# A feed-forward stage with quantized weights: dequantize before the matmul, or scale after it

## The chip, the cores and the metric

The kernel runs on one core of one Trainium2 chip. A core has five engines with queues of their own: TensorE (PE, matmuls into PSUM), VectorE (DVE), ScalarE (ACT), GpSimd (POOL, no PSUM here) and SyncE (SP, which issues the loads). The metric is the device time of the whole program in microseconds (us), lower is better. Before the change it is 1844.55 us, the median of three runs (1840.67 to 1845.38).

## What is computed

Two decoder layers on x of 8 batches x 128 tokens x 512 features: six sub-layers, each followed by a residual and a layer norm. The change is in the third, a feed-forward with weights kept as integers 0 to 15 and a zero and a scale for each group of 128 input features and each output column:

```
def dequantize(imatrix, scales, zeros, group_size, out_dtype):
    rs = jnp.repeat(scales, group_size, axis=0)
    rz = jnp.repeat(zeros, group_size, axis=0)
    return ((imatrix.astype(rs.dtype) - rz.astype(rs.dtype)) * rs).astype(out_dtype)
gate = jax.nn.silu(jnp.dot(x, gate_proj))      # 512 -> 1792
up = jnp.dot(x, up_proj)                        # 512 -> 1792
return jnp.dot(gate * up, down_proj)            # 1792 -> 512
x = _layernorm(x + _L0_ffn_ref(x, ...), axis=-1)
```

The group size 128 is also the depth of one matmul: 512 input features are four groups, c = 0 to 3.

## The kernel before

The program is six stages behind one another (hydra, cross0, ffn0, self, cross1, lora), with a barrier of all engines between them. The tokens stay in SBUF as m.xtok (tokens on partitions) and transposed as m.xT_hi and m.xT_lo, each number split into a high part of the matmul's reduced fp32 format and a low rest. `three` (L69 to 73) multiplies a high/low pair by a high/low pair with three matmuls and leaves out low times low.

The ffn0 stage (L1246, `ffn0_stage`) walks the 1792 inner features in 7 turns of 256. In a turn SP loads integers, zeros and scales of gate and up (six transfers of 512 KB, the zeros and scales copied to all partitions) and of down (three more). DVE subtracts the zeros (L1370, L1373), POOL multiplies by the scales (L1302, L1304), DVE makes the high part (L1378, L1383) and POOL the low part (L1308, L1310). A turn has four units: 128 inner features by 512 tokens each. In a unit PE runs the gate chain and the up chain, 4 groups x 3 matmuls each, into two pairs of banks; ACT takes silu of gate out of PSUM (L1352), DVE multiplies it by up (L1391, h), ACT copies the high part of h (L1358), DVE subtracts for the low part (L1396). After the four units PE multiplies h by the down weights, 8 batches x 2 halves of the turn x 3 matmuls of 512 columns, and DVE adds each batch's rows to m.xtok (L1405).

All turns after the first are a hardware loop on each engine. DVE's order in a turn sets when the weights of the next turn are made: behind the second unit. Semaphores name who waits for whom; nothing is scheduled by a planner.

At the end `norm_vector`, `norm_gpsimd`, `norm_tensor` and `norm_scalar` (L84 to 124) normalize: all eight batches' statistics, then one reciprocal root for all on POOL, then batch by batch scaling (DVE), transposing (PE), high copy (ACT), low subtraction (DVE). The cross0 stage before uses another form, one batch at a time: `batch_stats`, `batch_rstd`, `batch_scale`, `batch_turn`, `batch_high`, `batch_low` (L1428 to 1464).

m.pre is a buffer of 16 KB a partition for early loads. It serves the first two stages (`PREFETCHED = 2`, L1929) and is then given back. In cross0 SP loads the output weights in four parts into it, and POOL's splits (`split_q`, `split_o`) free it; its last use ends near 477 us, and that stage near 571.

## Time and profile before

| what | us |
|---|---|
| median of three runs | 1844.55 |
| the profiled execution, whole | 1839.86 |
| its span | 1838.0 |
| PE busy in the span | 1597.0 (87%) |
| DVE, ACT, POOL busy | 903.7, 726.9, 681.5 |
| ffn0: first load issued | 571.55 |
| ffn0: first matmul, last output row added | 598.98, 842.13 |
| ffn0: last low half of the norm | 861.55 |

Times inside the program count from the span's start. A matmul's busy time overlaps with its neighbours', since they are pipelined; the distance between their starts is what each costs. An operation on ACT, DVE or POOL also overlaps the next one of its engine a little. A time with an arrow behind it says how long the engine was idle before, and who ended the wait.

### The profile page before, as it was taken

How to read it: one execution, taken by the hardware profiler on the slowest of the kernel's cores; microseconds unless marked ns; L12 is line 12 of the kernel's file. 1: busy time of each engine (PE TensorE's matmuls, PEld its weight loads, DVE VectorE, ACT ScalarE, POOL GpSimd, SP SyncE). 2: the span in 40 equal slices, each digit the busy share in tenths (PEclk: the TensorE clock that was granted, in tenths of full speed). 3: DMA queues.
4: the chain of work that ended last, by engine and by line, in shares of the span. 5: the costliest groups of instructions: out<-in, count | busy, mean ns of one | idle time of the engine just before them, and what ended most of it. 6: DMA issues, size and time to landing. Idle time of an engine off the chain costs nothing. (4 is left out here: it accounts for less than half of the span.)

```text
span 1838.0 us, 29158 instructions
## 1 busy us (share of the span) xinstructions
PE 1597.0 (87%) x10870; PEld 1323.4 (72%) x10870; DVE 903.7 (49%) x1547; ACT 726.9 (40%) x2318; POOL 681.5 (37%) x498
## 2 busy tenths in 40 slices
PE   5888899999992999995699855999999999999846
PEld 3757687888871777773677634888888888888734
DVE  0726512333374455445256762555555555555744
ACT  2131224444441111111499952454445554445400
...
GB/s 189 35 0 0 49 13 26 19 34 5 2 2 140 169 103 166 142 0 62 82 1 2 47 8 120 26 34 47 35 36 31 28 47 35 24 1 1 1 41 46
DMA packets 70718, 84.93 MB, mean 46 GB/s; under 512 B 14080, under 2 KB 50304, under 8 KB 70592
## 3 DMA queue, kind: packets, MB, share of 16 engines
...
## 5 line engine op out<-in xcount | busy, mean ns | idle before, releaser
L984 POOL TENSOR_TENSOR xa_rs<-xa_ms,minus_half 128x5 f32<-128x5 f32 x64 | 74.8, 1169 | 171.1 <-DVE xa_ms L1206 171.1
L967 POOL TENSOR_TENSOR xa_prob<-xa_prob,xa_inv 128x512 f32<-128x512 f32 x64 | 66.6, 1041 | 138.7 <-DVE xa_inv L1173 138.7
L1151 ACT ACTIVATE xa_prob<-xa_prob,xa_peak 128x128 f32<-128x128 f32 x256 | 100.3, 394 | 42.5 <-DVE xa_peak L1217 42.5
L600 POOL TENSOR_TENSOR xa_prob<-xa_prob,xa_inv 128x1024 f32<-128x1024 f32 x32 | 60.7, 1896 | 141.2 <-DVE xa_inv L854 141.2
L1201 DVE TENSOR_REDUCE xa_ssq<-xa_qn 128x4 f32<-128x512 f32 x64 | 43.9, 686 | 136.7 <-ACT xa_qn L1137 136.7
L71 PE MATMUL xa_qp<-xa_q_hi,xT_hi 128*128 128x512 f32 x256 | 108.4, 423 | 2.0 <-DVE xa_q_lo L1164 2.0
L1741 ACT ACTIVATE sa_work<-sa_work,sa_peak 128x128 f32<-128x128 f32 x256 | 99.8, 399 | 21.2 <-DVE sa_peak L1778 21.1
L71 PE MATMUL xa_rows<-xa_o_hi,xa_out_hi 128*128 128x512 f32 x256 | 101.6, 397 | 5.2 <-DVE xtok L1180 5.2
L72 PE MATMUL xa_qp<-xa_q_hi,xT_lo 128*128 128x512 f32 x256 | 102.4, 400 | 0.0
L73 PE MATMUL xa_rows<-xa_o_lo,xa_out_hi 128*128 128x512 f32 x256 | 102.0, 398 | 0.0
L73 PE MATMUL xa_qp<-xa_q_lo,xT_hi 128*128 128x512 f32 x256 | 101.8, 398 | 0.0
L72 PE MATMUL xa_rows<-xa_o_hi,xa_out_lo 128*128 128x512 f32 x256 | 101.6, 397 | 0.0
L1577 POOL TENSOR_TENSOR sa_work<-sa_work,sa_inv 128x1024 f32<-128x1024 f32 x32 | 60.7, 1898 | 106.0 <-DVE sa_inv L1782 105.9
L1352 ACT ACTIVATE ff_act_g<-ff_gate 128x512 f32<-128x512 f32 x28 | 16.8, 600 | 209.8 <-PE ff_gate L73 209.8
L836 DVE TENSOR_REDUCE xa_peak<-xa_score 128x4 f32<-128x1024 f32 x32 | 39.2, 1224 | 114.3 <-PE xa_score L678 114.3
L1137 ACT ACTIVATE xa_qn<-xa_qp 128x512 f32<-128x512 f32 x64 | 38.3, 598 | 143.0 <-PE xa_qp L73 143.0
L71 PE MATMUL xa_kvp<-xa_kv_hi,cT_hi 128*128 128x256 f32 x256 | 78.7, 308 | 8.6 <-DVE xa_kv_lo L1159 8.6
L73 PE MATMUL xa_kvp<-xa_kv_lo,cT_hi 128*128 128x256 f32 x256 | 73.3, 286 | 0.0
L72 PE MATMUL xa_kvp<-xa_kv_hi,cT_lo 128*128 128x256 f32 x256 | 73.1, 286 | 0.0
L1034 PEld LDWEIGHTS xa_score<-xa_kT,xa_qT 128*128 128x128 f32 x512 | 66.9, 191 | 6.6 <-ACT xa_qT L1117 1.2
L71 PE MATMUL ff_gate<-xT_hi,ff_gu_hi 128*128 128x512 f32 x112 | 45.2, 404 | 29.8 <-POOL ff_gu_lo L1308 29.8
L1302 POOL TENSOR_TENSOR ff_gu_w<-ff_gu_w,ff_gu_s 128x2048 f32<-128x2048 f32 x7 | 37.8, 5398 | 86.2 <-DVE ff_gu_w L1370 86.2
...
## 6 DMA issues: line engine op xcount, KB each, us to landing
...
```

What stands on the lines that cost most here:

```text
L71: pe.matmul(out, a_hi, b_hi, start=first, stop=False)
L72: pe.matmul(out, a_lo, b_hi, start=False, stop=False)
L73: return pe.matmul(out, a_hi, b_lo, start=False, stop=last)
L600: pool.tensor_tensor(prob[:, t % 3, :, :], prob[:, t % 3, :, :], bc(inv[:, t % 3, :], 2, [P, Q, KEYS]), ALU.mult).then_inc(s["norm"], 1)
L836: dve.tensor_reduce(peak[:, t % 3, :], score4[:, :, 0:KEYS], AX, ALU.max, negate=True).then_inc(s["peak"], 1)
L967: pool.tensor_tensor(prob[:, u % 2, :, :], prob[:, u % 2, :, :], bc(inv[:, u % 2, :], 2, [P, Q, S]), ALU.mult).then_inc(s["norm"], 1)
L984: pool.tensor_tensor(rs[:, :], ms[:, :], m.minus_half[:, 0:Q + 1], ALU.pow).then_inc(s["rs"], 1)
L1034: last = pe.matmul(score[:, h * P:(h + 1) * P], qT[:, h, :], kT[:, :], start=True, stop=True)
L1151: last = act.activation(prob[:, u % 2, h, :], prob[:, u % 2, h, :], ACT.Exp, bias=peak[:, u % 2, h:h + 1], accum_out=total[:, u % 2, h:h + 1])
L1201: dve.tensor_reduce(ssq[:, 0:Q], qn[:, :, :], AX, ALU.add).then_inc(s["ssq"], 1)
L1577: pool.tensor_tensor(prob[:, u % 3, :, :], prob[:, u % 3, :, :], bc(inv[:, u % 3, :], 2, [P, HC, S]), ALU.mult).then_inc(s["norm"], 1)
L1741: last = act.activation(prob[:, t % 3, h, :], prob[:, t % 3, h, :], ACT.Exp, bias=peak[:, t % 3, h:h + 1], accum_out=total[:, t % 3, h:h + 1])
```

## The change

The gate and up weights are no longer scaled before the matmul. DVE subtracts the zeros and writes the integers (-15 to 15) straight into the matmul's format, where they are exact, so they need no low part. PE multiplies a group's integers by the high and the low x: 2 matmuls into a bank of their own, and so 8 groups a unit (4 gate, 4 up) in a ring of 6 banks. The scale of a group and an inner feature is then a column, one number a partition: the scales are loaded small and transposed once by PE (`sT`). ACT takes the even groups out of PSUM with the scale (`part`), DVE the odd ones with the scale and adds them to ACT's (`part`), POOL adds the two sums of gate and the two of up (`total`), ACT takes silu, POOL multiplies (`product`), ACT copies the high part (`high`), POOL subtracts the low part (`low`). The output rows of a turn are multiplied during the next turn's units, one batch in the middle of a unit and one at its end (`mid`, `end`), with the rest in `drain`; h therefore has two places, for which the idle m.cT buffers serve. The down weights are dequantized as before, but in smaller pieces. The loads of turn 0 are issued by SP in the cross0 stage into m.pre, which is kept one stage longer. The norm is done batch by batch. All hardware loops are written out.

The lines removed are the body of `ffn0_stage` as printed above. The lines added, with inner parts moved left, and without plain allocations:

```diff
+    ffn_scales(sp, io, m.scales, s["ld_next"])
+    sp.wait_ge(s["split_q"], PIECES_Q * Q)
+    sp.wait_ge(s["split_o"], PIECES_O * Q)
+    ffn_stage_inputs(sp, io, *ffn_stage_buffer(m.pre), 0, s["ld_next"])
+    sp.wait_ge(s["ld_next"], 96)
...
+def ffn_stage_inputs(sp, io, dest_q, dest_z, g, done):
+    cols = slice(g * WIDE, (g + 1) * WIDE)
+    for n, w in enumerate(("gate", "up")):
+        sp.dma_start(dest_q[:, :, n, :], io[w + "_w"].rearrange("(c p) n -> p c n", p=P)[:, :, cols]).then_inc(done, 16)
+        sp.dma_start(dest_z[:, :, n, :], io[w + "_z"][:, cols].partition_broadcast(P)).then_inc(done, 16)
+def ffn_stage_buffer(flat):
+    return [flat[:, n * KC * 2 * WIDE:(n + 1) * KC * 2 * WIDE].bitcast(INT32).rearrange("p (c a n) -> p c a n", c=KC, a=2) for n in range(2)]
+def ffn_scales(sp, io, dest, done):
+    for n, w in enumerate(("gate", "up")):
+        sp.dma_start(dest[n * KC * TILES:(n + 1) * KC * TILES, :], io[w + "_s"].rearrange("g (t n) -> (g t) n", n=P)).then_inc(done, 16)
 def ffn0_stage(nc, m, io, sem):
+    UNITS = 4 * TURNS
+    RING = 6
+    LAST = TURNS - 1
...
+        other = sb("other", [P, 2 * KC * 2 * WIDE])
+        stage = [ffn_stage_buffer(m.pre), ffn_stage_buffer(other)]
+        w = sb("w", [P, 2, KC, 2, WIDE], F32R)
...
+        acc = sb("acc", [P, 2, 4, HALF])
...
+        dn_hi, dn_lo = (sb(n, [P, 2, MT, D], F32R) for n in ("dn_hi", "dn_lo"))
+        h_hi, h_lo = (x[:, :, :].rearrange("p (a k) n -> p a k n", a=2) for x in (m.cT_hi, m.cT_lo))
...
+        mid, end, drain = {}, {}, []
+        for n in range(4, 4 * LAST):
+            g, j = n // 4, n % 4
+            mid[n], end[n] = [(g - 1, 2 * j)], [(g - 1, 2 * j + 1)]
+        n = 4 * LAST
+        for j in range(2):
+            mid[n + j] = [(LAST - 1, 4 * j), (LAST - 1, 4 * j + 1)]
+            end[n + j] = [(LAST - 1, 4 * j + 2), (LAST - 1, 4 * j + 3)]
+        end[n + 2], mid[n + 3], end[n + 3] = [(LAST, 0)], [(LAST, 1)], [(LAST, 2)]
+        drain = [(LAST, b) for b in range(3, B)]
+        def column(n, i):
+            t = MT * (n // 4) + n % MT
+            return sT[:, i // 4, i % 4, t:t + 1]
...
 @block.sync
...
+    for g in range(TURNS):
+        if g:
+            if g >= 3:
+                sp.wait_ge(s["w"], KC * (g - 2))
+            elif g == 2:
+                sp.wait_ge(s["w_first"], KC)
+            ffn_stage_inputs(sp, io, *stage[g % 2], g, s["ld_odd" if g % 2 else "ld_even"])
+            sp.wait_ge(s["dn_sub"], g)
+            sp.wait_ge(s["dn_w"], MT * g)
...
+        sp.dma_start(dn_q[:, :, :], io["down_w"].rearrange("(m p) n -> p m n", p=P)[:, part, :]).then_inc(s["ld_dn"], 16)
...
 @block.gpsimd
...
+    def low(n):
+        g, half, k = n // 4, n % 4 // 2, n % MT
+        cols = slice(half * HALF, (half + 1) * HALF)
+        pool.wait_ge(s["h_hi"], n + 1)
+        pool.tensor_tensor(h_lo[:, g % 2, k, cols], acc[:, n % 2, 2, :], raw(h_hi[:, g % 2, k, cols]),
+                           ALU.subtract).then_inc(s["h_lo"], 1)
+    def total(n, a):
+        pool.wait_ge(s["cd"], 4 * n + 2 + 2 * a)
+        pool.tensor_tensor(acc[:, n % 2, 2 * a, :], acc[:, n % 2, 2 * a, :], acc[:, n % 2, 2 * a + 1, :], ALU.add).then_inc(s["sum"], 1)
+    def product(n):
+        pool.wait_ge(s["silu"], n + 1)
+        pool.wait_ge(s["sum"], 2 * n + 2)
+        pool.tensor_tensor(acc[:, n % 2, 2, :], acc[:, n % 2, 0, :], acc[:, n % 2, 2, :], ALU.mult).then_inc(s["h"], 1)
+    for n in range(UNITS):
+        g, j = n // 4, n % 4
+        if n:
+            low(n - 1)
+        total(n, 0)
+        if j == 0:
+            pool.wait_ge(s["dn_sub"], g + 1)
+            for k in range(MT):
+                pool.tensor_tensor(dn_w[:, k, :], dn_w[:, k, :], dn_s[:, k, :], ALU.mult).then_inc(s["dn_w"], 1)
+        total(n, 1)
+        product(n)
+    low(UNITS - 1)
+    for b in range(B):
+        batch_rstd(pool, m, n2, b)
 @block.tensor
...
+    def group(n, i):
+        q = 8 * n + i
+        g, half, k, c, a = n // 4, n % 4 // 2, n % MT, i % 4, i // 4
+        cols = slice(half * HALF, (half + 1) * HALF)
+        if q >= RING:
+            pe.wait_ge(s["cd"] if i % 2 else s["ca"], (q - RING) // 2 + 1)
+        elif q == RING - 1:
+            pe.wait_ge(s["sT"], 1)
+        f = slice(k * P, (k + 1) * P)
+        bank = ring[q % RING]
+        pe.matmul(bank[:, :], w[:, g % 2, c, a, f], m.xT_hi[:, c, cols], start=True, stop=False)
+        pe.matmul(bank[:, :], w[:, g % 2, c, a, f], m.xT_lo[:, c, cols], start=False, stop=True).then_inc(s["grp"], 1)
+    def out_rows(g, b):
+        r = B * g + b
+        half = b // 4
+        pe.wait_ge(s["dn_lo"], MT * (g + 1))
+        pe.wait_ge(s["h_lo"], 4 * g + 2 * (half + 1))
+        if r >= 2:
+            pe.wait_ge(s["add"], r - 1)
+        for k in range(MT):
+            last = three(pe, rows[r % 2][:, :], h_hi[:, g % 2, k, b * P:(b + 1) * P], h_lo[:, g % 2, k, b * P:(b + 1) * P],
+                         dn_hi[:, g % 2, k, :], dn_lo[:, g % 2, k, :], k == 0, k == MT - 1)
+        last.then_inc(s["rows"], 1)
+    def turn(b):
+        if b == 0:
+            pe.wait_ge(s["cd"], 4 * UNITS)
+            pe.wait_ge(s["ca"], 4 * UNITS)
+        if b >= 2:
+            pe.wait_ge(n2["lo"], b - 1)
+        batch_turn(pe, m, n2, b, ring[b % 2][:, :])
+    pe.transpose(ring[RING - 1][:, 0:2 * KC * TILES], m.scales[0:2 * KC * TILES, :],
+                 m.ident[0:2 * KC * TILES, 0:2 * KC * TILES]).then_inc(s["sT_mm"], 1)
+    for n in range(UNITS):
+        g, j = n // 4, n % 4
+        if n == 0:
+            pe.wait_ge(s["w_first"], KC)
+        elif j == 0:
+            pe.wait_ge(s["w"], KC * g)
+        for i in range(4):
+            group(n, i)
+        for r in mid.get(n, ()):
+            out_rows(*r)
+        for i in range(4, 8):
+            group(n, i)
+        for r in end.get(n, ()):
+            out_rows(*r)
+    for n, r in enumerate(drain):
+        out_rows(*r)
+        if n:
+            turn(n - 1)
+    for b in range(len(drain) - 1, B):
+        turn(b)
 @block.scalar
...
+    def part(n, i):
+        act.wait_ge(s["grp"], 8 * n + i + 1)
+        act.activation(acc[:, n % 2, i // 2, :], ring[(8 * n + i) % RING][:, :], ACT.Copy, scale=column(n, i)).then_inc(s["ca"], 1)
+    def high(n):
+        g, half, k = n // 4, n % 4 // 2, n % MT
+        act.wait_ge(s["h"], n + 1)
+        if g >= 2:
+            act.wait_ge(s["rows"], B * (g - 1))
+        act.activation(h_hi[:, g % 2, k, half * HALF:(half + 1) * HALF], acc[:, n % 2, 2, :], ACT.Copy).then_inc(s["h_hi"], 1)
+    act.wait_ge(s["sT_mm"], 1)
+    act.activation(sT[:, :, :, :].rearrange("p a c t -> p (a c t)"), ring[RING - 1][:, 0:2 * KC * TILES], ACT.Copy).then_inc(s["sT"], 1)
+    act.wait_ge(s["sT"], 1)
+    for n in range(UNITS):
+        g, j = n // 4, n % 4
+        if n >= 2:
+            act.wait_ge(s["h_lo"], n - 1)
+        part(n, 0)
+        part(n, 2)
+        if n:
+            high(n - 1)
+        if j == 1:
+            for k in range(MT):
+                act.wait_ge(s["dn_w"], MT * g + k + 1)
+                if g >= 2 and k == 0:
+                    act.wait_ge(s["rows"], B * (g - 1))
+                act.activation(dn_hi[:, g % 2, k, :], dn_w[:, k, :], ACT.Copy).then_inc(s["dn_hi"], 1)
+        act.wait_ge(s["sum"], 2 * n + 1)
+        act.activation(acc[:, n % 2, 0, :], acc[:, n % 2, 0, :], ACT.Silu).then_inc(s["silu"], 1)
+        part(n, 4)
+        part(n, 6)
+    high(UNITS - 1)
+    for b in range(B):
+        batch_high(act, m, n2, b, ring[b % 2][:, :])
 @block.vector
...
+    def part(n, i):
+        dve.wait_ge(s["grp"], 8 * n + i + 1)
+        dve.wait_ge(s["ca"], 4 * n + i // 2 + 1)
+        dve.scalar_tensor_tensor(acc[:, n % 2, i // 2, :], ring[(8 * n + i) % RING][:, :], column(n, i), acc[:, n % 2, i // 2, :],
+                                 ALU.mult, ALU.add).then_inc(s["cd"], 1)
+    def add_rows(g, b):
+        r = B * g + b
+        dve.wait_ge(s["rows"], r + 1)
+        if g:
+            dve.wait_ge(s["add"], r - B + 1)
+        dve.tensor_tensor(m.xtok[:, b, :], m.xtok[:, b, :], rows[r % 2][:, :], ALU.add).then_inc(s["add"], 1)
+    q, z = stage[0]
+    for c in range(KC):
+        dve.tensor_tensor(w[:, 0, c, :, :], q[:, c, :, :], z[:, c, :, :], ALU.subtract).then_inc(s["w_first"], 1)
+    dve.wait_ge(s["sT"], 1)
+    for n in range(UNITS):
+        g, j = n // 4, n % 4
+        for r in end.get(n - 1, ()):
+            add_rows(*r)
+        if j == 0:
+            dve.wait_ge(s["ld_dn"], 48 * (g + 1))
+            if g:
+                dve.wait_ge(s["dn_lo"], MT * g)
+            dve.tensor_tensor(dn_w[:, :, :], dn_q[:, :, :], dn_z[:, :, :], ALU.subtract).then_inc(s["dn_sub"], 1)
+        part(n, 1)
+        part(n, 3)
+        if g < LAST:
+            q, z = stage[(g + 1) % 2]
+            if j == 0:
+                dve.wait_ge(s["ld_even" if g % 2 else "ld_odd"], 64 * ((g + 1) // 2 if g % 2 else g // 2 + 1))
+                dve.wait_ge(s["grp"], 32 * g)
+            dve.tensor_tensor(w[:, (g + 1) % 2, j, :, :], q[:, j, :, :], z[:, j, :, :], ALU.subtract).then_inc(s["w"], 1)
+        for r in mid.get(n, ()):
+            add_rows(*r)
+        part(n, 5)
+        part(n, 7)
+        if j == 1:
+            for k in range(MT):
+                dve.wait_ge(s["dn_hi"], MT * g + k + 1)
+                dve.tensor_tensor(dn_lo[:, g % 2, k, :], dn_w[:, k, :], raw(dn_hi[:, g % 2, k, :]), ALU.subtract).then_inc(s["dn_lo"], 1)
+    for r in end[UNITS - 1]:
+        add_rows(*r)
+    for b in range(B):
+        if b >= 3:
+            add_rows(LAST, b)
+        if b >= 5:
+            batch_low(dve, m, n2, b - 5, ring[(b - 5) % 2][:, :])
+        dve.wait_ge(s["add"], B * LAST + b + 1)
+        batch_stats(dve, m, n2, b)
+        if b:
+            batch_scale(dve, m, n2, b - 1)
+    batch_scale(dve, m, n2, B - 1)
+    for b in range(3, B):
+        batch_low(dve, m, n2, b, ring[b % 2][:, :])
...
-PREFETCHED = 2
+PREFETCHED = 3
```

## Rows read from the trace of the kernel before

**Rows 1.** table by stretches: length, busy (count) by engine, PE clock, DMA share, GB/s

```profile
540.00:566.00 26.00, 19.72 (x244) 15.29 (x244) 17.41 (x30) 9.23 (x19) 5.92 (x6) 1.00 0.01 2
...
566.00:599.00 33.00, 0.64 (x5) 0.44 (x5) 14.36 (x10) 1.88 (x2) 12.75 (x4) 0.56 0.65 211
...
735.00:770.00 35.00, 33.78 (x148) 27.43 (x147) 19.10 (x21) 4.60 (x8) 15.38 (x4) 1.00 0.42 140
...
842.00:862.00 20.00, 8.39 (x32) 5.86 (x32) 14.78 (x34) 4.79 (x8) 1.65 (x1) 0.60 0.00 0
```

**Rows 2.** groups by line, 530 to 920 us: busy, mean ns, idle before

```profile
L71 PE MATMUL ff_gate<-xT_hi,ff_gu_hi 128*128 128x512 f32 x112 | 45.2, 404 | 29.8 <-POOL ff_gu_lo L1308 29.8
...
L1358 ACT ACTIVATE ff_h_hi<-ff_h 128x512 fp32r<-128x512 f32 x28 | 17.6, 628 | 16.8 <-DVE ff_h L1391 16.8
...
L1569 POOL TENSOR_TENSOR xtok<-xtok,sa_bias_o 128x512 f32<-128x512 f32 x8 | 9.8, 1267 | 0.0
```

**Rows 3.** timeline, the stage's start: start, us, engine, line

```profile
571.55 0.39 SPq L1283 DMA_DIRECT2D ff_gu_q<-in_gate_w  x1
...
583.20 2.29 DVE L1370 TENSOR_TENSOR ff_gu_w<-ff_gu_q,ff_gu_z 128x2048 f32<-128x2048 int32 x1 [12.66 <-DMA ff_gu_s<-in_up_s]
...
587.03 4.11 DVE L1373 TENSOR_TENSOR ff_dn_w<-ff_dn_q,ff_dn_z 128x1024 f32<-128x1024 int32 x1 [1.54 <-DMA ff_dn_s<-in_down_s]
...
600.00 0.63 PE L73 MATMUL ff_gate<-xT_lo,ff_gu_hi 128*128 128x512 f32 x1
...
600.43 0.63 PE L71 MATMUL ff_gate<-xT_hi,ff_gu_hi 128*128 128x512 f32 x1
```

**Rows 4.** the product h of the feed-forward (ff_h): ns min/median/max, first and last start

```profile
L1391 DVE TENSOR_TENSOR ff_h<-ff_act_g,ff_up x28: 686/687/689, 607.1 to 830.2; 128x512 f32<-128x512 f32 x28
```

**Rows 5.** timeline, ACT in a turn, last high half, last low half

```profile
747.56 0.60 ACT L1352 ACTIVATE ff_act_g<-ff_gate 128x512 f32<-128x512 f32 x1 [4.89 <-PE ff_gate L73]
...
748.05 0.63 ACT L1358 ACTIVATE ff_h_hi<-ff_h 128x512 fp32r<-128x512 f32 x1
...
830.94 0.64 ACT L1358 ACTIVATE ff_h_hi<-ff_h 128x512 fp32r<-128x512 f32 x1 [2.40 <-DVE ff_h L1391]
...
860.86 0.69 DVE L100 TENSOR_TENSOR xT_lo<-ff_gate,xT_hi 128x512 fp32r<-128x512 f32 x1 [0.36 <-ACT xT_hi L122]
```

**Rows 6.** timeline, POOL with 128x512 operations

```profile
265.49 1.04 POOL L564 TENSOR_TENSOR xa_wide_hi<-pre,ones 128x512 fp32r<-128x512 f32 x1 [39.55 <-PE xa_score L73]
...
266.61 1.30 POOL L566 TENSOR_TENSOR xa_wide_lo<-pre,xa_wide_hi 128x512 fp32r<-128x512 f32 x1
...
893.29 9.84 POOL L1569 TENSOR_TENSOR xtok<-xtok,sa_bias_o 128x512 f32<-128x512 f32 x8
```

**Rows 7.** timeline, the norm of one batch

```profile
566.09 0.69 DVE L1430 BATCH_NORM_STATS2 stats<-xtok 128x6 f32<-128x512 f32 x1
...
567.04 0.15 DVE L1434 TENSOR_SCALAR var<-meanvar 128x1 f32<-128x1 f32 x1
...
567.27 0.55 POOL L1439 TENSOR_TENSOR rstd<-var,minus_half 128x1 f32<-128x1 f32 x1 [5.39 <-DVE var L1434]
...
567.86 0.55 DVE L1444 TENSOR_SCALAR xtok<-xtok,meanvar,rstd 128x512 f32<-128x512 f32 x1 [0.66 <-POOL rstd L1439]
```

**Rows 8.** groups by line, ACT: a copy without and with a column of scales

```profile
L1126 ACT ACTIVATE xa_v_hi<-xa_kvp 128x128 fp32r<-128x128 f32 x64 | 17.3, 270 | 0.0
...
L356 ACT ACTIVATE hy_yT<-hy_bank,hy_norm_w 128x128 f32<-128x128 f32 x32 | 9.5, 366 | 7.2 <-PE hy_bank L306 6.8
```

**Rows 9.** timeline, DVE and POOL in one turn

```profile
753.77 1.22 DVE L1373 TENSOR_TENSOR ff_dn_w<-ff_dn_q,ff_dn_z 128x1024 f32<-128x1024 int32 x1
...
753.93 5.55 POOL L1302 TENSOR_TENSOR ff_gu_w<-ff_gu_w,ff_gu_s 128x2048 f32<-128x2048 f32 x1 [10.85 <-DVE ff_gu_w L1370]
...
756.46 3.57 DVE L1396 TENSOR_TENSOR ff_h_lo<-ff_h,ff_h_hi 128x512 fp32r<-128x512 f32 x1
...
759.45 2.86 POOL L1304 TENSOR_TENSOR ff_dn_w<-ff_dn_w,ff_dn_s 128x1024 f32<-128x1024 f32 x1
```

More of the change, by code:

```diff
@@ L1258, in ffn0_stage @@
+        acc = sb("acc", [P, 2, 4, HALF])
         dn_q, dn_z = (sb(n, [P, MT, D], INT32) for n in ("dn_q", "dn_z"))
         dn_s, dn_w = (sb(n, [P, MT, D]) for n in ("dn_s", "dn_w"))
-        dn_hi, dn_lo = (sb(n, [P, MT, D], F32R) for n in ("dn_hi", "dn_lo"))
-        act_g = sb("act_g", [P, 2, HALF])
-        h = sb("h", [P, 2, HALF])
-        h_hi, h_lo = (sb(n, [P, MT, TOK], F32R) for n in ("h_hi", "h_lo"))
-        gate = [pb(f"gate{i}") for i in range(2)]
-        up = [pb(f"up{i}") for i in range(2)]
+        dn_hi, dn_lo = (sb(n, [P, 2, MT, D], F32R) for n in ("dn_hi", "dn_lo"))
@@ L1266, in ffn0_stage @@
+        h_hi, h_lo = (x[:, :, :].rearrange("p (a k) n -> p a k n", a=2) for x in (m.cT_hi, m.cT_lo))
+        ring = [pb(f"ring{i}") for i in range(RING)]
         rows = [pb(f"rows{i}") for i in range(2)]
-        m.norm_bank = gate
         s = {n: sem("ff_" + n) for n in (
-            "ld_gu", "ld_dn", "sub_gu", "sub_dn", "w_gu", "w_dn", "hi_gu", "hi_dn", "lo_gu", "lo_dn", "gate",
-            "up", "silu", "h", "h_hi", "h_lo", "rows", "add")}
+            "ld_even", "ld_odd", "ld_dn", "w_first", "w", "sT_mm", "sT", "grp", "ca", "cd", "sum", "silu", "h", "h_hi", "h_lo",
+            "dn_sub", "dn_w", "dn_hi", "dn_lo", "rows", "add")}
@@ L1297, in _ @@
             @block.gpsimd
             def _(pool):
-                def scale(g):
-                    pool.wait_ge(s["sub_gu"], g + 1)
-                    pool.tensor_tensor(gu_w[:, :, :, :], gu_w[:, :, :, :], gu_s[:, :, :, :], ALU.mult).then_inc(s["w_gu"], 1)
-                    pool.wait_ge(s["sub_dn"], g + 1)
-                    pool.tensor_tensor(dn_w[:, :, :], dn_w[:, :, :], dn_s[:, :, :], ALU.mult).then_inc(s["w_dn"], 1)
-                def low(g):
-                    pool.wait_ge(s["hi_gu"], g + 1)
-                    pool.tensor_tensor(gu_lo[:, :, :, :], gu_w[:, :, :, :], raw(gu_hi[:, :, :, :]), ALU.subtract).then_inc(s["lo_gu"], 1)
-                    pool.wait_ge(s["hi_dn"], g + 1)
-                    pool.tensor_tensor(dn_lo[:, :, :], dn_w[:, :, :], raw(dn_hi[:, :, :]), ALU.subtract).then_inc(s["lo_dn"], 1)
@@ L1312, in _ @@
-                scale(0)
-                low(0)
-                with pool.Fori(1, TURNS) as g:
-                    scale(g)
-                    low(g)
-                norm_gpsimd(pool, m, n2)
+                def low(n):
[4 more added lines that the diff above has]
+                                       ALU.subtract).then_inc(s["h_lo"], 1)
@@ L1319, in _ @@
+                low(UNITS - 1)
+                for b in range(B):
+                    batch_rstd(pool, m, n2, b)
             @block.tensor
             def _(pe):
-                def group(g):
-                    pe.wait_ge(s["lo_gu"], g + 1)
-                    for j in range(CHAINS):
-                        half, k = j // MT, j % MT
-                        cols = slice(half * HALF, (half + 1) * HALF)
-                        pe.wait_ge(s["h"], CHAINS * g + max(j - 1, 0))
-                        for n, (bank, done) in enumerate(((gate[j % 2], s["gate"]), (up[j % 2], s["up"]))):
-                            for c in range(KC):
-                                last = three(pe, bank[:, :], gu_hi[:, c, n, k * P:(k + 1) * P], gu_lo[:, c, n, k * P:(k + 1) * P],
-                                             m.xT_hi[:, c, cols], m.xT_lo[:, c, cols], c == 0, c == KC - 1)
-                            last.then_inc(done, 1)
-                    pe.wait_ge(s["lo_dn"], g + 1)
-                    for b in range(B):
-                        pe.wait_ge(s["h_lo"], CHAINS * g + MT * (b // 4 + 1))
-                        pe.wait_ge(s["add"], B * g + max(b - 1, 0))
-                        for k in range(MT):
-                            last = three(pe, rows[b % 2][:, :], h_hi[:, k, b * P:(b + 1) * P], h_lo[:, k, b * P:(b + 1) * P],
-                                         dn_hi[:, k, :], dn_lo[:, k, :], k == 0, k == MT - 1)
-                        last.then_inc(s["rows"], 1)
@@ L1346, in _ @@
+                for n, r in enumerate(drain):
[4 more added lines that the diff above has]
+                    turn(b)
             @block.scalar
             def _(act):
-                def group(g):
-                    for j in range(CHAINS + 1):
-                        if j < CHAINS:
-                            act.wait_ge(s["gate"], CHAINS * g + j + 1)
-                            act.activation(act_g[:, j % 2, :], gate[j % 2][:, :], ACT.Silu).then_inc(s["silu"], 1)
-                        if j:
-                            n = j - 1
-                            half, k = n // MT, n % MT
-                            act.wait_ge(s["h"], CHAINS * g + n + 1)
-                            act.wait_ge(s["rows"], B * g)
-                            act.activation(h_hi[:, k, half * HALF:(half + 1) * HALF], h[:, n % 2, :], ACT.Copy).then_inc(s["h_hi"], 1)
```

85 lines of the change are left out of this document (7 added, 78 removed).

## The prediction

> **What bounds the kernel now.** I read the table by stretches first, to see what the feed-forward stage is made of, then the groups by line, then the timelines of its start, one turn, and its end. The table [rows 1] shows four parts: 33 us in which PE works 0.64 us, a body in which PE is busy 33.78 of 35 us at the full clock, and 20 us at the end with PE busy 8.4. PE in the body is the bound: 148 matmuls in 33.78 us are 0.228 us each, and a turn of 144 makes 32.9 of its roughly 34.4. Every other engine there is at most 19 of 35 busy. The hole at the start ends with POOL: PE waited 29.8 us for ff_gu_lo [rows 2]. Its inside is the load, from 571.55 to 583.20, then subtract, scale, split and scale again in a row [rows 3]. The first product h begins at 607.1 and the last at 830.2, 27 units of (128 features x 512 tokens) later, 8.26 us each [rows 4]; the last low half of the norm ends at 861.55 [rows 5].
>
> **PE's share after the change.** A unit has 8 groups of 2 matmuls instead of 2 chains of 12, and still 12 for the output rows: 28 instead of 36. That is 28 x 0.228 = 6.4 us instead of 8.2, and over 28 units 51 us less. If PE stayed the bound, this would be the gain. I do not think it does, for the scales now cost ACT, DVE and POOL work on every group, and the order written for them closes a ring.
>
> **The ring.** Follow one unit from the end of product(n-1) on POOL. ACT does high(n-1); POOL may only then do low(n-1), and after it, in its order, total(n,0); ACT waits for that with silu(n) and only behind silu issues part(n,4) and part(n,6); DVE adds part(n,7); POOL does total(n,1) and product(n). Nothing in it can start a unit earlier, since each engine's order is fixed. The two parts 0 and 2 and DVE's 1 and 3 are done before and cost nothing. Prices:
> - high: 0.63 for SBUF to SBUF [rows 2], 0.04 from DVE's end (830.21 + 0.69) to ACT's start at 830.94 [rows 4, 5], taken for POOL to ACT as well: 0.67.
> - low and total(n,0): a 128x512 tensor operation of two SBUF operands on POOL is 1.26 [rows 2], and eight in a row took 9.84, so 1.225 from one start to the next. A POOL operation that waits for another engine starts 0.08 after that one's end (567.19 to 567.27) [rows 6, 7]. So 0.08 + 1.225 + 1.26 = 2.57.
> - silu, part 4, part 6: ACT's 128x512 takes 0.60 and the next starts 0.49 later [rows 5]. What a scale taken from a column adds is not shown at this size; at 128x128 it makes 366 ns of 270 [rows 8], so 0.10. Its cost lies between 0 and 0.2 a part; I take 0.10. So 0.04 + 0.53 + 0.60 + 0.70 = 1.87.
> - part 7 on DVE: 0.04 + 0.70, the 0.69 of a PSUM operation at this size [rows 4] and 0.01 for the column.
> - total(n,1): 0.08 + 1.26; product, which waits for POOL's own total: 1.12 from start to start where the operation took 1.04 [rows 6], so 0.08 + 1.25. Together 2.67.
> Sum: 0.67 + 2.57 + 1.87 + 0.74 + 2.67 = 8.5 us a unit. That is longer than PE's 6.4 and longer than the 8.26 of now. PE gets 2 us of idle per unit. With no column cost and every hand-over at its least it is 8.2, with 0.03 more at each of nine hand-overs 8.8.
>
> **What else is in a turn of four units.** POOL's two multiplications of dn_w (2 x 1.25) fall between total 0 and total 1, where POOL waits 2.7 us for ACT and DVE anyway: nothing. ACT's dn_hi falls in its wait for total 0: nothing. DVE's own sum is 4 parts, 2 additions of rows, 1 subtraction and a quarter of the dn work, some 5.4 of 8.5: not the bound. But DVE and POOL exclude one another when DVE has two SBUF operands: DVE's h_lo, 0.69 at other times, started at 756.46 and took 3.57, to 0.55 after POOL's 5.55 us operation ended at 759.48; and POOL's own next one, at 759.45, and that one before it, which met a DVE subtraction at 753.77, were each longer than their work [rows 9]. So DVE slips in between two POOL operations and pushes the later one. The new subtraction w (once a unit) is asked for 0.9 before product ends, waits, and runs in the 0.75 us while ACT does high: no cost. The dn subtraction (1.1 us, first unit of a turn) comes between total 1 and product: +1.05. The two dn_lo (second unit) come around total 1: +0.45 and +0.55, and the w after them meets low: +0.25. In 7 turns: 6 x 1.05 + 7 x 1.25 = 15. The bounds are 0, if every one falls into one of POOL's gaps, and 30, if all 24 w (0.6), 6 dn (1.1) and 14 dn_lo (0.6) displace POOL, less the first turn.
>
> **Start.** SP begins at 571.55 as now [rows 3], since the 2 MB of integers for turn 0 and the scales come in the stage before, behind the last weights, and land long before its end; PE there does not wait for them. DVE subtracts at once, PE can begin at 574. But DVE's order blocks it: before part 1 stands the dn load, three 512 KB transfers; they would be there at about 579.4, one step of three before the six and nine below. Then dn subtraction and parts 1 and 3, to 582. Then the w subtraction, which waits for turn 1's four transfers, the seventh in the queue; six were there at 583.20 and nine at 587.03, so 584.5 [rows 3]. Subtraction 0.6, parts 5 and 7 1.3, total and product 2.67: product(0) ends at 589.0. PE's cold start (0.43 us a matmul, 600.00 to 600.43) is hidden in that. Bounds 586 and 592.
>
> **End.** After product(27): high and low 2.1. Only then may POOL do rstd(0), for low stands ahead of it: 0.55 more. From there DVE is the chain. A batch costs it stats, aggregate and var 1.1, scale 0.55 [rows 7], row addition and low half 0.65 each: 2.95 in full. So 2.65 + 0.55 for scale 0, 1.6 for batch 1 and 2's rest, 2.25 twice, 2.95 three times, 1.2 for the last rstd and scale, 1.3 for two low halves that are ready, and 3.8 for the last three at the pace of transpose, copy and subtraction: 24.5. Now it is 30.7 from 830.9 to 861.55 [rows 4, 5]. Bounds 20 and 28.
>
> **Sum.** 589.0 + 27 x 8.52 (230) + 15 + 24.5 = 858.6 against 861.55: 3 us less. Loads in the stage before, longer straight code in place of loops, SP's longer list: nothing on the path, at most 2 us either way. The profiled execution has a span of 1838.0 and 1839.86 in all, 4.7 below the median 1844.55 of three; less 3 it is 1836.9, and on the median's scale 1841.6. I say 1841.
>
> **Rivals.**
> A. DVE never hurts POOL and the hand-overs are at their least: 27 x 8.2 = 221 instead of 245, and some 1 to 3 us off start and end: 22 to 28 us faster than my sum, 1815. For it: the w subtraction has 0.15 us of room by my own schedule, and if the dn ones found such room too, the 15 are gone. Against: the two waits in [rows 9]. Chance 0.20.
> B. PE is the bound after all: 589 + 27 x 6.4 + 24.5 = 786: 75 us faster, 1769. It needs the ring to be under 6.4; its four POOL operations make 5.0, and ACT's high and silu 1.2 more before any part. Chance 0.06.
> C. Slower: POOL loses to DVE on every two-operand subtraction. Place: the hand-over between POOL's back-to-back operations in each unit; price 0.6 a unit and 1.1 a turn; it decides as soon as the w subtraction misses the 0.75 us hole while ACT does high, which happens if DVE reaches it 0.2 us later than I have it. Then 30 instead of 15, and with 8.7 in place of 8.52 another 5: 20 us more than my sum, 1861. Chance 0.24.
> D. PE's clock. PE will idle 2 of 8.5 us. Where it was busy 19.72 of 26 us, the same share, the clock was 1.00 [rows 1]. At half clock a unit is 28 x 0.427 = 12 us, longer than the ring: +96 if always, +24 if a quarter of the time, 1865. Chance 0.04. The Trainium skill, "TensorE: Matmul & The Clock Gate", section "A second HAM failure mode: psum-queue depth-cycling", says that a kernel that cycles through PSUM banks at 512 columns made TensorE idle briefly between groups and its clock swing between the levels. The new ring of six banks is of that kind; the 26 us row at 1.00 speaks against it.
> That the change does not do what it says: the hole at the start surely shrinks, so this would be a matter of the body alone, and is in C.
>
> **How the numbers follow.** My case has 0.46 and its own range is 1830 to 1852 (start 3, ring 8, contention 8, end 4, added as independent). A measurement of this kernel tells 0.3% (5.5 us) from nothing. Faster: A and B, 0.26, and 0.17 of mine. Same: 0.22 of mine and 0.04 at the edge of A and C. Slower: the rest, 0.31. The range takes in A and C: 1808 to 1862.
>
> **What would show it.** Right: ff products one ring of about 8.5 us apart with PE idle about 2 of it at a clock of 1.00, POOL busy some 5 to 5.5 of each 8.5 us and ACT's silu waiting for POOL; the second product some 8.5 us behind a first that ends near 589; 24 us between the last product and the last low half. Wrong: units 6.4 us apart with PE never idle (B), subtractions of 0.69 us throughout (A), POOL operations of 1.8 us in most units (C), a clock under 0.9 in the body (D), or parts on ACT other than 0.7.

## The result, and the profile after

The changed kernel takes 1845.41 us (median of 20 runs, 1843.74 to 1849.91) where the kernel before takes 1843.02 (median of 20, 1840.63 to 1846.27). The ratio is 1.0016, with an interval of 1.0009 to 1.0023: 2.4 us slower by the medians, 3 us by the ratio. I had forecast 3 us faster. The difference is within the 0.3% that I called no change, but it is clearly on the other side of zero. The interesting part is what lies under this small number: PE has 51 us less to do in the stage, and nothing of it arrives.

The table by stretches of the changed kernel (length, busy time and count of PE, weight loads, DVE, ACT, POOL, then PE's clock, DMA share, GB/s) stands against [rows 1]:

```profile
540.00:566.00 26.00, 19.01 (x236) 14.64 (x228) 17.50 (x28) 8.77 (x18) 5.61 (x6) 1.00 0.01 2
...
589.00:626.00 37.00, 24.96 (x75) 17.29 (x74) 17.36 (x25) 15.45 (x26) 24.60 (x19) 0.82 0.25 77
663.50:700.00 36.50, 29.29 (x111) 20.62 (x110) 23.19 (x31) 15.46 (x26) 24.24 (x18) 0.95 0.30 98
700.00:738.00 38.00, 30.90 (x117) 21.94 (x116) 24.67 (x33) 15.35 (x26) 25.47 (x19) 0.96 0.30 103
845.00:864.00 19.00, 10.89 (x51) 7.99 (x49) 15.58 (x34) 4.79 (x8) 4.15 (x6) 0.77 0.00 0
```

In the body PE is busy 29.29 of 36.5 us where it was busy 33.78 of 35 [rows 1], with 111 matmuls instead of 148; a matmul takes 0.264 us of PE's busy time instead of 0.228, at a granted clock of 0.95 instead of 1.00. No engine is full: PE is busy 80% of the stretch, POOL 66% and DVE 64%. That is the picture of a ring, and the products, one a unit, give its length:

```profile
L1342 POOL TENSOR_TENSOR ff_acc<-ff_acc x56: 1262/1286/2194, 580.7 to 837.6; 128x512 f32<-128x512 f32 x56
L1347 POOL TENSOR_TENSOR ff_acc<-ff_acc x28: 1262/1538/2090, 587.8 to 839.0; 128x512 f32<-128x512 f32 x28
```

The row gives least, median and largest duration in ns, and the first and last start. From 587.84 to 839.02 there are 27 units of 9.30 us, against 8.26 before [rows 4]. The table of waits (who waited for whom: us in all, times, longest) between 589 and 840 us shows all three engines of the ring waiting once a unit for the one ahead of them, and PE waiting for ACT to empty a bank:

```profile
DVE ff_acc L1465 <- ACT ff_acc L1426: 97.7, 28, 5.7
ACT cT_hi L1433 <- POOL ff_acc L1347: 79.4, 27, 4.4
ACT ff_acc L1453 <- POOL ff_acc L1342: 66.5, 27, 3.1
POOL ff_acc L1342 <- DVE ff_acc L1465: 61.6, 27, 2.8
...
PE ff_ring L1376 <- ACT ff_acc L1426: 37.4, 21, 3.4
```

A collision is an operation of DVE and one of POOL, each with two SBUF operands, at the same time; one of the two then takes longer. One unit without a collision that costs POOL time, in the timeline (start, duration, engine, line, what ended the wait before it):

```profile
692.62 0.64 ACT L1433 ACTIVATE cT_hi<-ff_acc 128x512 fp32r<-128x512 f32 x1 [3.39 <-POOL ff_acc L1347]
692.69 0.68 DVE L1495 TENSOR_TENSOR ff_w<-pre 128x512 fp32r<-128x512 int32 x1
...
693.33 1.30 POOL L1337 TENSOR_TENSOR cT_lo<-ff_acc,cT_hi 128x512 fp32r<-128x512 f32 x1 [0.74 <-ACT cT_hi L1433]
...
694.59 1.28 POOL L1342 TENSOR_TENSOR ff_acc<-ff_acc 128x512 f32<-128x512 f32 x1
...
695.89 0.63 ACT L1453 ACTIVATE ff_acc<-ff_acc 128x512 f32<-128x512 f32 x1 [2.64 <-POOL ff_acc L1342]
696.43 2.41 ACT L1426 ACTIVATE ff_acc<-ff_ring,ff_sT 128x512 f32<-128x512 f32 x4
...
697.15 0.50 PE L1376 MATMUL ff_ring<-xT_hi,ff_w 128*128 128x512 f32 x1 [1.92 <-ACT ff_acc L1426]
697.20 1.41 DVE L1465 SCALAR_TENSOR_TENSOR ff_acc<-ff_ring,ff_sT,ff_acc 128x512 f32<-128x512 f32 x2 [3.24 <-ACT ff_acc L1426]
...
698.69 1.30 POOL L1342 TENSOR_TENSOR ff_acc<-ff_acc 128x512 f32<-128x512 f32 x1 [0.36 <-DVE ff_acc L1465]
700.13 1.30 POOL L1347 TENSOR_TENSOR ff_acc<-ff_acc 128x512 f32<-128x512 f32 x1
...
701.46 0.63 ACT L1433 ACTIVATE cT_hi<-ff_acc 128x512 fp32r<-128x512 f32 x1 [2.62 <-POOL ff_acc L1347]
```

From one high half to the next are 8.84 us. The group of four on ACT is parts 4 and 6 of this unit and 0 and 2 of the next. PE's row shows where its 2 us of idle come from: the ring of six banks is full until ACT takes part 4.

The other units have the same path. Read one by one from the timeline, eight of the 27 last 8.79 to 8.85 us, and each of the others is longer, to within 0.1 us, by what POOL's own low, total or product took beyond 1.3 us. Silu and parts 4 and 6 take 1.82 us in all 27, without a wait for PE.

The start and the end of the stage, from the timeline, stand against [rows 3] and [rows 5]:

```profile
570.85 2.50 DVE L1477 TENSOR_TENSOR ff_w<-pre 128x512 fp32r<-128x512 int32 x4 [1.02 <-PEq L2054]
578.09 1.23 DVE L1487 TENSOR_TENSOR ff_dn_w<-ff_dn_q,ff_dn_z 128x1024 f32<-128x1024 int32 x1 [4.75 <-DMA ff_dn_s<-in_down_s]
...
583.96 1.05 DVE L1495 TENSOR_TENSOR ff_w<-ff_other 128x512 fp32r<-128x512 int32 x1 [3.32 <-DMA ff_other<-in_up_z]
...
863.13 0.69 DVE L1562 TENSOR_TENSOR xT_lo<-ff_ring,xT_hi 128x512 fp32r<-128x512 f32 x1 [0.99 <-ACT xT_hi L1557]
```

The first product ends at 589.38 and not at 607.8, the last low half of the norm ends at 863.82 against 861.55 [rows 5], 23.5 us after the last product instead of 30.7. So the start gives 18 us, the end 7, and the body takes 28 back.

### The profile page after: what moved, and what is told of

It reads as the page before. It is cut to its first block and busy times, and to the rows that moved or that the text cites. A ratio compares the mean times of both kernels' runs of the same rounds, so it can differ in the third digit from the quotient of the medians.

```text
span 1842.0 us, 28850 instructions
## 1 busy us (share of the span) xinstructions
PE 1577.0 (86%) x10647; PEld 1286.6 (70%) x10647; DVE 935.0 (51%) x1631; ACT 801.8 (44%) x2445; POOL 752.5 (41%) x603
## 3 DMA queue, kind: packets, MB, share of 16 engines
q1 hardware_dynamic: 60860, 74.36, 12.9%
## 5 line engine op out<-in xcount | busy, mean ns | idle before, releaser
L1376 PE MATMUL ff_ring<-xT_hi,ff_w 128*128 128x512 f32 x224 | 101.2, 452 | 52.8 <-ACT ff_acc L1426 39.1
L1465 DVE SCALAR_TENSOR_TENSOR ff_acc<-ff_ring,ff_sT,ff_acc 128x512 f32<-128x512 f32 x112 | 78.7, 744 | 97.7 <-ACT ff_acc L1426 97.7
L1376 PEld LDWEIGHTS ff_ring<-xT_hi,ff_w 128*128 128x128 f32 x224 | 46.1, 206 | 87.6 <-ACT ff_acc L1426 49.9
L1342 POOL TENSOR_TENSOR ff_acc<-ff_acc 128x512 f32<-128x512 f32 x56 | 75.4, 1347 | 77.1 <-DVE ff_acc L1465 77.1
L1377 PE MATMUL ff_ring<-xT_lo,ff_w 128*128 128x512 f32 x224 | 94.0, 419 | 0.0
```

Source lines behind the costliest of these rows:

```text
L1342: pool.tensor_tensor(acc[:, n % 2, 2 * a, :], acc[:, n % 2, 2 * a, :], acc[:, n % 2, 2 * a + 1, :], ALU.add).then_inc(s["sum"], 1)
L1376: pe.matmul(bank[:, :], w[:, g % 2, c, a, f], m.xT_hi[:, c, cols], start=True, stop=False)
L1377: pe.matmul(bank[:, :], w[:, g % 2, c, a, f], m.xT_lo[:, c, cols], start=False, stop=True).then_inc(s["grp"], 1)
L1465: dve.scalar_tensor_tensor(acc[:, n % 2, i // 2, :], ring[(8 * n + i) % RING][:, :], column(n, i), acc[:, n % 2, i // 2, :], ALU.mult, ALU ...
```

## The experiments

A ratio below is to the kernel before the change, which was timed beside each experiment; the changed kernel's own ratio is 1.0016. Differences in us are to the changed kernel's 1845.41. The kernel before took 1842.06 us beside e1 to e4 and 1843.14 beside e5 to e8, so such a difference is good to about 1 us.

My theory: the body is bound by one ring, POOL to ACT to POOL to ACT to DVE to POOL, whose length is set by the order that is written for POOL and ACT, and PE's work is off the path. The first rival: PE with its ring of banks binds it. The second: POOL's conflicts with DVE make the length.

**e1: POOL's order alone.** The low half moves out of the ring's first part.

```
 for n in range(UNITS):
-    if n: low(n - 1)
     total(n, 0)
     if j == 0: (dn_w multiplications)
+    if n: low(n - 1)
     total(n, 1); product(n)
```

> Only POOL's order is changed: low(n-1) stands behind total(n,0) and the dn multiplications instead of ahead of total(n,0). Ring theory (a unit is 8.84 us because product, high, low, total 0, silu, parts 4 and 6, part 7, total 1, product follow one another): high and low leave the ring, total 0 starts right at product's end, a unit without contention is 1.26 + 0.57 + 0.58 + 0.69 + 0.92 + 1.38 + 1.44 = 6.85, a turn about 30.4 us instead of 37.2, the program 1799 us (1790 to 1808). Rival, PE or its banks or clock set the pace: no change, 1845 within 3. Rival, collisions between DVE and POOL on SBUF set it: at most the 12 us that they cost in all, 1833.

Measured: 1810.9 us, ratio 0.9822 (0.9779 to 0.9864). Faster by 34 us with the same instructions, as only the ring theory has it, but 12 us less than I expected of it. The products go from 589.4 to 807.4, 8.07 us a unit instead of 9.30: 1.23 less, where I expected 1.7. Two things take the rest. Totals now meet DVE's subtractions more often: 28 of them take over 1.4 us, where 8 did.

```profile
L1342 POOL TENSOR_TENSOR ff_acc<-ff_acc x56: 1260/1482/2212, 582.3 to 806.0; 128x512 f32<-128x512 f32 x56
```

The median total is 1.48 us here and 1.29 in the changed kernel, the least is 1.26 in both. Between the first and the last product, all of POOL's operations together run 18.7 us over 1.29 each, against 12.9 in the changed kernel: 6 of the 12 us. And total 0 doesn't always start right at product's end. In 13 of the 27 units it waits for DVE's parts 1 and 3, which stand behind DVE's work for the unit before, 9.3 us in all, as here (the product, then total 0):

```profile
660.98 1.54 POOL L1347 TENSOR_TENSOR ff_acc<-ff_acc 128x512 f32<-128x512 f32 x1
663.38 1.67 POOL L1342 TENSOR_TENSOR ff_acc<-ff_acc 128x512 f32<-128x512 f32 x1 [0.86 <-DVE ff_acc L1465]
```

The two together cover the 12 us.

**e2: ACT's order alone.** Parts 4 and 6 go ahead of high and silu, so that ACT's and DVE's parts leave the ring.

```
     part(n, 0); part(n, 2)
+    part(n, 4); part(n, 6)
     if n: high(n - 1)
     ...
     act.activation(... ACT.Silu)
-    part(n, 4); part(n, 6)
```

> Only ACT's order is changed: parts 4 and 6 stand right behind parts 0 and 2, ahead of high and silu. Ring theory: silu, both parts and DVE's part 7 leave the ring, which is high, low, total 0, total 1 and product, 0.66 + 0.08 + 1.26 + 1.29 + 1.29 + 0.14 + 1.30 = 6.0 us, with the dn multiplications no longer hidden 6.6 on average and 7.1 with collisions: a turn of 28.5 us, the program 1786 us (1776 to 1800). Rival, PE sets the pace: no change, 1845 within 3. Rival, collisions: 1833.

Measured: 1803.64 us, ratio 0.978 (0.9737 to 0.9822): 42 us less than the changed kernel's 1845.41, 18 less gain than expected. The products go from 590.6 to 796.3, 7.62 us each. In most units POOL's timeline has the form that I expected, four operations in a row with only high between; then, in the last unit of a turn, a new wait appears. It is ACT's high, which is ready by its data but stands behind parts that wait for PE:

```profile
688.61 1.28 POOL L1337 TENSOR_TENSOR cT_lo<-ff_acc,cT_hi 128x512 fp32r<-128x512 f32 x1 [0.74 <-ACT cT_hi L1433]
689.84 2.53 POOL L1342 TENSOR_TENSOR ff_acc<-ff_acc 128x512 f32<-128x512 f32 x2
692.52 1.30 POOL L1347 TENSOR_TENSOR ff_acc<-ff_acc 128x512 f32<-128x512 f32 x1
696.52 1.29 POOL L1337 TENSOR_TENSOR cT_lo<-ff_acc,cT_hi 128x512 fp32r<-128x512 f32 x1 [2.71 <-ACT cT_hi L1433]
```

ACT in the same stretch:

```profile
694.32 0.69 ACT L1426 ACTIVATE ff_acc<-ff_ring,ff_sT 128x512 f32<-128x512 f32 x1 [1.38 <-PE ff_ring L1377]
695.24 0.69 ACT L1426 ACTIVATE ff_acc<-ff_ring,ff_sT 128x512 f32<-128x512 f32 x1 [0.23 <-PE ff_ring L1377]
695.82 0.62 ACT L1433 ACTIVATE cT_hi<-ff_acc 128x512 fp32r<-128x512 f32 x1
```

In all, POOL's low waits 35.9 us for high between 591 and 797, where it waits 20.0 in the changed kernel between 589 and 840, and these 16 us are most of the 18 that are missing; the collisions cost hardly more than there (13.9 us over 1.29 each). Part of the 16 is PE's clock, a rival that I hadn't named for this run. PE idles 1.66 us before 686.04, and then its granted clock falls for about 3 us, here in the table by stretches:

```profile
688.00:691.00 3.00, 3.00 (x8) 2.32 (x8) 2.93 (x5) 0.53 (x1) 2.39 (x2) 0.50 1.05 331
691.00:695.00 4.00, 4.00 (x18) 3.28 (x18) 2.53 (x4) 2.46 (x4) 2.67 (x3) 1.00 0.00 1
```

The clock of 0.50 is the lower of its two levels, 1.2 GHz. Seven distances between matmuls in a row are 0.43 us there instead of 0.23, and PE doesn't idle again before ACT has waited for it. That is 1.4 us of the 2.0 by which this wait is longer than the others, and it recurs in four turns, at 657, 688, 718 and 749: some 6 us, an estimate from these distances. No run holds the clock up in this order.

**e3: both orders** (the two edits above together).

> Both orders changed, as in the two others. Ring theory: no ring is left that is longer than PE's own work; POOL has 4 x 1.26 and a quarter of 2.5 us a unit, 5.8 with collisions 6.3, PE 28 x 0.23 = 6.4: a turn of 26 to 27.5 us, the program 1772 us (1765 to 1785). Rival, PE or its clock already sets the pace: 1845 within 3.

Measured: 1785.2 us, ratio 0.9681 (0.9639 to 0.9723), 60 us less than the changed kernel, 7.14 us a unit. The same instructions, in another order on two engines, beat both kernels. A stretch of its body in the table, and its totals:

```profile
660.00:690.00 30.00, 28.92 (x123) 22.53 (x123) 25.05 (x35) 18.16 (x30) 28.46 (x21) 1.00 0.35 123
```

```profile
L1342 POOL TENSOR_TENSOR ff_acc<-ff_acc x56: 1260/1673/2361, 584.4 to 782.9; 128x512 f32<-128x512 f32 x56
```

POOL is busy 28.46 of 30 us, and now a collision costs its full price, because POOL has no gap left to fall into: here DVE's dn subtraction and a total start together, at 663.20 and 663.24. DVE's row, then POOL's:

```profile
663.20 1.21 DVE L1487 TENSOR_TENSOR ff_dn_w<-ff_dn_q,ff_dn_z 128x1024 f32<-128x1024 int32 x1
```

```profile
663.24 2.33 POOL L1342 TENSOR_TENSOR ff_acc<-ff_acc 128x512 f32<-128x512 f32 x1
```

The total takes 2.33 us instead of 1.28, and it ends 1.16 after the subtraction: POOL stood still for 1.05 us. From the first to the last product, POOL's operations run 21.6 us over 1.29 each; the expectation had 0.5 a unit for this, 13.5, so it is 8 of the 13 us by which it missed. The rest lies in the last turn. The first 24 units last 6.9 us on average, but the third from the end 9.1 and the last 11.7. In the one PE has four batches of output rows to multiply instead of two. Ahead of the other's groups stand rows that need h of the same turn, and so POOL's low, which now comes later. The low ends at 771.21, PE starts the rows at 771.31, ACT waits for PE and POOL for DVE:

```profile
769.94 1.27 POOL L1337 TENSOR_TENSOR cT_lo<-ff_acc,cT_hi 128x512 fp32r<-128x512 f32 x1
```

```profile
775.16 0.69 ACT L1426 ACTIVATE ff_acc<-ff_ring,ff_sT 128x512 f32<-128x512 f32 x1 [4.51 <-PE ff_ring L1377]
```

```profile
778.43 1.29 POOL L1342 TENSOR_TENSOR ff_acc<-ff_acc 128x512 f32<-128x512 f32 x1 [4.56 <-DVE ff_acc L1465]
```

PE's granted clock is at the lower level here too:

```profile
771.00:777.00 6.00, 5.69 (x14) 4.46 (x15) 1.44 (x2) 0.88 (x2) 2.73 (x3) 0.50 0.00 0
```

**e4: half of the group matmuls.** In the changed kernel, PE's second matmul of each group goes.

```
-    pe.matmul(bank[:, :], w[...], m.xT_hi[...], start=True, stop=False)
-    pe.matmul(bank[:, :], w[...], m.xT_lo[...], start=False, stop=True).then_inc(s["grp"], 1)
+    pe.matmul(bank[:, :], w[...], m.xT_hi[...], start=True, stop=True).then_inc(s["grp"], 1)
```

> The second matmul of each group, with the low part of x, is left out: 224 matmuls of 512 columns less, which is 8 x 0.23 = 1.84 us a unit. The output is not the reference's. Ring theory: PE only idles more, the time stays within 3 us of 1845. Rival, PE, its clock or its banks set the pace: up to 28 x 1.84 = 51 us faster, 1794.

Measured: 1843.95 us, ratio 1.0006 (0.9987 to 1.0026). 224 matmuls less, 51 us of PE at 0.228 each, change nothing, and the products still go from 589.2 to 839.5, 9.27 us each:

```profile
L1347 POOL TENSOR_TENSOR ff_acc<-ff_acc x28: 1263/1530/2095, 589.2 to 839.5; 128x512 f32<-128x512 f32 x28
```

The first rival is out: PE's work is not on the path. This is the plainest answer to where PE's 51 us went. It also settles the clock for the changed kernel's order, since PE's clock fell here and the unit stayed as long:

```profile
630.00:660.00 30.00, 18.18 (x64) 12.25 (x62) 18.55 (x24) 11.04 (x19) 18.86 (x15) 0.94 0.26 90
660.00:690.00 30.00, 21.30 (x64) 14.85 (x65) 18.96 (x26) 14.20 (x25) 18.51 (x14) 0.83 0.38 123
```

**e5: the norm of before.** The changed kernel's body with the old norm behind the last output row.

```
-    for b in range(B): batch_rstd(pool, m, n2, b)
+    norm_gpsimd(pool, m, n2)
     (likewise norm_tensor, norm_scalar, norm_vector for the batchwise ones)
```

> The changed kernel with the norm of before at the stage's end (all statistics, one reciprocal root, then the batches). From the trace of the changed kernel the last product ends at 840.3 and the last low half at 863.8, 23.5 us. With the norm of before the rows of batches 4 to 7 are added some 8 us after the last product, and the norm takes 19.4 us from there as it did before: 27.8 us. So 4 us slower than the changed kernel, 1849 (1847 to 1852). If the old norm were as good, 1845.

Measured: 1852.03 us, ratio 1.0056 (1.0042 to 1.0069). Its last product ends at 842.28 and its last low half at 871.94: 29.7 us, where I expected 27.8 and the changed kernel has 23.5. The time is at the end of the range.

```profile
871.25 0.69 DVE L100 TENSOR_TENSOR xT_lo<-ff_ring,xT_hi 128x512 fp32r<-128x512 f32 x1 [0.36 <-ACT xT_hi L122]
```

So the norm batch by batch brings 6 us by the trace, 7 by the ratios.

**e6: turn 0 loaded in the stage.** Integers and scales are loaded where the stage starts, as before the change, and not in the stage ahead.

```
 @block.sync                       (cross-attention stage ahead)
-    ffn_scales(...); ffn_stage_inputs(..., 0, s["ld_next"])
 @block.sync                       (feed-forward)
+    ffn_scales(...); ffn_stage_inputs(..., 0, s["ld_next"])
```

> The changed kernel with turn 0's integers and scales loaded at the start of the feed-forward stage, ahead of the other loads. Four more transfers of 512 KB stand ahead of the dn load and of turn 1's, which is what part 5 of the first unit waits for: at the pace of six by 583.2 and nine by 587.0 they add 5.1 us. So the first product ends at 594.5 instead of 589.4 and the program takes 1850.5 us (1848 to 1853). Rival: the early load is what filled the hole of 29.8 us, and without it most of that comes back: 1860 or more.

Measured: 1853.76 us, ratio 1.0055 (1.0043 to 1.0067), 0.8 us above the range, and not the rival's 1860 or more. The first product ends at 597.03 and not at 594.5.

```profile
581.13 2.50 DVE L1476 TENSOR_TENSOR ff_w<-pre 128x512 fp32r<-128x512 int32 x4 [10.48 <-DMA pre<-in_up_z]
585.17 1.23 DVE L1486 TENSOR_TENSOR ff_dn_w<-ff_dn_q,ff_dn_z 128x1024 f32<-128x1024 int32 x1 [1.55 <-DMA ff_dn_s<-in_down_s]
```

DVE is idle 10.48 us for the load instead of 1.02. Its idle starts at 570.65 and the first product at 595.49, which is 24.8 us later, where the changed kernel takes from 569.83 to 587.84, 18.0. So the early load brings 7 us, by this and by the ratios, and not the 9.5 of the wait alone, for the wait for the dn load behind it is 1.55 us instead of 4.75.

**e7: fewer collisions.** From the third turn on, DVE's subtractions for the down weights cover 32 of 512 columns.

```
+    few = D if g < 2 else 32
-    dve.tensor_tensor(dn_w[:, :, :], dn_q[:, :, :], dn_z[:, :, :], ALU.subtract)
+    dve.tensor_tensor(dn_w[:, :, 0:few], dn_q[:, :, 0:few], dn_z[:, :, 0:few], ALU.subtract)
     (the same for dn_lo)
```

> From turn 2 on DVE's two subtractions for the down weights (zeros, low part) run over 32 of 512 columns, so that the output is not the reference's; POOL's and ACT's work on them is whole. What collisions of DVE and POOL cost: they make a turn 37.2 us where four units without them make 35.4. The five turns then are 1.5 to 1.9 us shorter each: 8 to 9 us faster than the changed kernel, 1837 (1834 to 1840). If collisions were free because the ring has room for them, 1845.

Measured: 1835.15 us, ratio 0.9959 (0.9947 to 0.9971), 10 us less than the changed kernel. Its products are 8.97 us apart (590.2 to 832.5), and the last 21 units each last 8.80 to 8.87, the clean unit's 8.84. The collisions of the down weights cost some 10 us: real, but a sixth of the 60 us that the two orders cost.

**e8: less for POOL.** e3, and DVE adds the gate's parts 2 and 3 onto the same sum, so that POOL's first total goes.

```
-    total(n, 0)                                (POOL)
-    part(n, 2)                                 (ACT)
+    part(n, 2)                                 (DVE, onto acc[:, n % 2, 0, :])
     silu waits for DVE's part 3 instead of POOL's total
```

> On top of both orders changed (1785 us, where POOL is busy 28.5 of 30 us): group 2 of the gate is added by DVE onto the same sum instead of by ACT into a second one, and POOL's total of the gate is gone. POOL has three operations and a quarter of 2.5 us, 4.5 us a unit, with collisions 5.2; DVE five parts, two rows, a subtraction and the dn work, 6.3; PE 6.4. If POOL is what bounds the kernel with both orders, a unit falls from 7.5 to 6.7 us and the program to 1764 (1758 to 1775). If PE's order (groups behind output rows) bounds it, 1785 within 4; if DVE does, above 1780.

Measured: 1782.99 us, ratio 0.9666 (0.965 to 0.9682), not to be told from e3's 0.9681, with 6.93 us a unit.

```profile
660.00:690.00 30.00, 29.04 (x125) 22.93 (x124) 28.45 (x40) 15.14 (x26) 21.25 (x16) 1.00 0.38 123
```

POOL fell from 28.46 to 21.25 of 30 us and the time hardly moved. PE is busy 29.04 of 30, DVE 28.45, and ACT's longest account is now a wait for PE (68.5 us in 58 waits between 600 and 775). In the order with both edits PE is close enough behind POOL that taking 7 us of 30 from POOL only makes PE and DVE the bound; which of the two it is, this run does not tell apart.

## Why the prediction was wrong

Its mechanism held, and its sum missed by 5.2 us of stage on a forecast gain of 3. By its own steps, to the stage's end (858.6 forecast, 863.82 measured):

- **Start.** Product(0) forecast to end at 589.0, ended at 589.38: +0.4. The dn load blocked DVE as said (forecast to land at 579.4, DVE went on at 578.09), the fourth load of turn 1 too (584.5, 583.96).
- **The ring: this is the step that failed, the size of the 8.5 us a unit.** A clean unit is 8.84 where the sum had 8.52 and its own upper bound was 8.8, and 27 times the difference is 8.6 us, more than the whole forecast gain. Term by term, from the clean unit above, product's end at 692.58 to product's end at 701.43 (ACT's four parts start (2.41 - 0.684) / 3 = 0.575 apart, so part 6 ends at 697.69): high 0.68 (forecast 0.67); low and total 0 2.61 (2.57); silu and parts 4 and 6 1.82 (1.87); part 7 on DVE 0.92 (0.74); total 1 and product 2.82 (2.67). Two terms carry it. Part 7 ends 0.92 after ACT's part 6 and not 0.74. I priced it from ACT's end, but part 5 stands ahead of it on DVE: it starts 0.09 behind ACT's part 4, at 697.20, and part 7 follows 0.67 later, at 697.87. Half of the 0.18 is this wait for part 5; the hand-over from ACT to DVE, 0.09 and not 0.04, and the operation, 0.74 and not 0.70, are the other half. And a product that waits for POOL's own total starts 0.14 after its end (837.61 + 1.27 = 838.88, then 839.02), not 0.08, and POOL's operations took 1.28 to 1.30, not 1.25. The column scale on ACT, my unknown, was right: 0.684 for 0.70.
- **Collisions.** Forecast 15 us. From the first product's end (589.38) to the last's (840.28) are 250.9 us; less 27 x 8.84 = 238.7 that leaves 12.2: -2.8. In a turn of the body the dn subtraction costs POOL 0.8 us (forecast 1.05), the two dn_lo 0.6 together (1.0), and the w after them 0.5 (0.25). In the other units w cost nothing, as said: it found the hole while ACT does high (692.69), or DVE waited and POOL did not (700.44, 1.53 us). e7 confirms the size. Of the hidden operations, the dn_w multiplications and dn_hi cost nothing, as said.
- **End.** 24.5 forecast, 23.5 measured: -1.
- **Span.** These make 864 against 861.55, +2.3 us, in a stage that starts 0.7 us earlier. The span rose by 4.0; of the other 1.7, 0.3 lie before the next stage's first matmul (874.42 against 871.78), and the rest was not traced further. The medians rose by 2.4.

Rival A (no collisions, hand-overs at their least, 1815) fell on both counts. B (PE the bound, 1769) is excluded by e4; its gain exists only with the other orders, and there it falls short of its 75 us: e3 has 60, and e8, which also moves work, 62. C (POOL loses every time, 1861): it loses sometimes, 12 us and not 30. D: the clock did go to 0.95 and, in the first 37 us, to 0.82, where I expected 1.00. It cost nothing in this order of operations, since no piece of the path waits for PE and e4 at 0.83 takes the same time; in e2 and at the end of e3, where the path does wait for PE, it did. By the rule of the Trainium skill that I cited there, "TensorE: Matmul & The Clock Gate", section "A second HAM failure mode: psum-queue depth-cycling", a kernel of this kind swings between clock levels. The changed kernel's trace agrees: its granted clock is 0.50 from 679.5 to 682 and 1.00 from 683 to 716. But e1, e3 and e8 have the same ring of six banks, and their clock stays at 1.00 from 630 to 720, so the ring of banks alone does not bring the swing.

What I did not see in the forecast is how loose the kernel is. I had worked out that the ring is 2 us longer than PE's need, and took the order as given; a move of three calls (low, part 4, part 6) was worth 20 times the net effect that I was trying to size. And a forecast gain of 3 us out of bounds for the ring alone of 8.2 to 8.8 us a unit, 16 us over 27 units, could not carry its sign.

In the expectations of e1 to e3 I then made the opposite error: I took a term out of the ring and left the others as they were. What was late next was of three kinds: more collisions (median total 1.29, 1.48, 1.67 us in the changed kernel, e1 and e3); an engine that issues in order and comes late with the next thing asked of it (DVE's parts in e1, ACT's high behind a part that waits for PE in e2); and PE itself, once the others no longer hide it, with its clock at the lower level for 3 us a turn in e2 and in the last turn of e3.
